# Building a graph's adjacency from one-hots on two engines instead of one

## What is computed

```python
def _genconv(x, src, dst, t, w1, b1, lg, lb, w2, b2):
    m = jax.nn.relu(x[src]) + EPS
    z = m * t
    ...
    e = jnp.exp(z - zmax[dst])
    denom = jax.ops.segment_sum(e, dst, num_segments=N)
    alpha = e / (denom[dst] + 1e-16)
    agg = jax.ops.segment_sum(alpha * m, dst, num_segments=N)
    h = agg + x
    h = jax.nn.relu(_ln(h @ w1 + b1, lg, lb))
    return h @ w2 + b2
```

## Time and profile before

| what | us |
|---|---|
| median of 3 runs (990.37 to 992.57) | 990.45 |
| the profiled execution: its own time | 991.27 |
| the profiled execution: its span | 989.4 |
| first one-hot written, from the span's start | 113.04 |
| weights of the last pair of one-hot matmuls | 201.72 |
| first aggregation of layer 0 | 211.94 |
| TensorE busy, share of the span | 92% |

### The profile page before, as it was taken

How to read it: one execution, slowest core, us unless ns; L and a number is a source line. 1 busy time by engine, 2 the same in 40 slices (tenths; PEclk the granted TensorE clock), 3 DMA queues, 4 the chain that set the end, 5 groups by cost and what they waited for, 6 DMA issues and landing times. The chain is left out here.

```text
span 989.4 us, 13105 instructions
## 1 busy us (share of the span) xinstructions
PE 912.4 (92%) x4281; PEld 666.8 (67%) x4281; DVE 707.1 (71%) x1315; ACT 445.3 (45%) x696; POOL 380.6 (38%) x326
## 2 busy tenths in 40 slices
PE   5998999979999999989999989799999999999970
PEld 3997544448887778867788777566666666666640
DVE  6856789966654676777767888588677766677765
ACT  2665000052634535435264244566565666666630
POOL 2003000016600454105531153667766666766630
PEclk9999999979999999999999999999999999999995
DMA  6433000033200222012110263599999999999868
GB/s 176 145 121 122 18 1 0 0 117 128 86 1 7 89 86 86 1 54 85 52 61 11 74 224 128 161 331 325 339 340 354 349 329 355 357 356 325 285 176 204
DMA packets 57161, 159.73 MB, mean 161 GB/s; under 512 B 13901, under 2 KB 21651, under 8 KB 48656
## 3 DMA queue, kind: packets, MB, share of 16 engines
q1 hardware_dynamic: 44725, 147.50, 43.4%
q0 software_dynamic: 12288, 11.36, 4.2%
q10 hardware_dynamic: 91, 0.13, 0.1%
HBM read 152.71 MB, written 25.58 MB: 180 GB/s over the span
## 5 line engine op out<-in xcount | busy, mean ns | idle before, releaser
L259 PE MATMUL ps<-split_operands 128*125 128x512 f32 (+5 forms) x690 | 266.2, 386 | 16.2 <-DVE split_operands L1256 5.4
L260 PE MATMUL ps<-split_operands 128*125 128x512 f32 (+5 forms) x690 | 260.4, 377 | 0.0
L261 PE MATMUL ps<-split_operands 128*125 128x512 f32 (+5 forms) x690 | 260.1, 377 | 0.0
L653 POOL DMA_INDIRECT yrow_scratch<-work,row_i x64 | 151.6, 2369 | 95.4 <-ACT work L953 92.8
L259 PEld LDWEIGHTS ps<-split_operands 128*125 128x125 f32 (+3 forms) x690 | 129.5, 188 | 45.3 <-issue 9.6
L1470 DVE TENSOR_TENSOR gate_up_lo<-expert_weights,split_operands 128x2048 fp32r<-128x2048 f32 x64 | 147.0, 2297 | 0.5 <-ACT split_operands L935 0.5
L261 PEld LDWEIGHTS ps<-split_operands 128*125 128x125 f32 (+3 forms) x690 | 129.5, 188 | 26.5
L391 POOL TENSOR_TENSOR split_operands<-work,split_operands 128x512 fp32r<-128x512 f32 x66 | 83.5, 1293 | 162.0 <-ACT split_operands L373 153.1
L260 PEld LDWEIGHTS ps<-split_operands 128*125 128x125 f32 (+3 forms) x690 | 129.6, 188 | 23.6
L935 ACT ACTIVATE split_operands<-expert_weights 128x2048 fp32r<-128x2048 f32 x64 | 121.8, 1903 | 0.0
L1963 PE MATMUL ps<-expert_weights,work 128*117 128x512 f32 x256 | 120.3, 592 | 0.5 <-issue 0.5
(11 more groups left out here) (217 smaller groups left out, 1242.5 us busy)
## 6 DMA issues: line engine op xcount, KB each, us to landing
expert_weights<-experts_in SPq DMA_DIRECT2D x64, 1024.0 KB
expert_weights<-experts_in SPq DMA_DIRECT2D x64, 512.0 KB
work<-w_in SPq DMA_DIRECT2D x12, 1024.0 KB, 5.1
yrow_scratch<-work SPq DMA_DIRECT2D x5, 1500.0 KB
split_operands<-yrow_scratch SPq DMA_DIRECT2D x4, 1120.0 KB
work<-cw_in SPq DMA_DIRECT2D x3, 1024.0 KB, 5.2
work<-rows_in SPq DMA_DIRECT2D x10, 256.0 KB, 4.6
work<-wmix_in SPq DMA_DIRECT2D x4, 512.0 KB, 5.4
```

Source lines behind the costliest of these rows:

```text
L259: pe.matmul(o, a[1], b[0], start=start, stop=False)
L260: pe.matmul(o, a[0], b[1], start=False, stop=False)
L261: return pe.matmul(o, a[0], b[0], start=False, stop=stop)
L653: pool.indirect_dma_start(yrow, bass.IndirectOffsetOnAxis(ap=row_i[:, e:e + 1], axis=0), OS[e % 4], None, bounds_check=last_row, oob_is_er ...
```

## The change

The change does five things.

1. In each group the fifth source one-hot is made by ScalarE, as Relu(1 - Abs(source - node)): an Abs of 125x626 into a new buffer `apart`, then a Relu of 125x626 into the slot. VectorE makes the other four and all five destination one-hots. TensorE waits for both engines at the fifth slot. ScalarE waits for the slot to be free before it starts Abs.
2. One pair of semaphores counts slots through all tiles; the running number of groups before a tile (`before`) is made by four more one-element steps in `tile_ranges`, and every engine loads it for tiles 1 to 4. The first group of a tile stands outside the loop, and ScalarE's copies of the tile before stand behind it.
3. The buffers `srcf`, `dstf`, `iota_h` move off EP's place; the cast that makes `iota_h` moves from the kernel's start to the other preparations of the edges.
4. The global maximum is made early. ScalarE makes the exponentials of source tiles 0 and 1 and their high parts before the adjacency; what VectorE and ScalarE have to do for these two tiles stands between the last steps of the adjacency.
5. TensorE waits for `adj_lo` only ahead of the destination tiles 2 to 4.

```diff
-        srcf, dstf = [fg(12288 + 2 * CH * i, 2 * CH, p=T) for i in range(2)]
-        iota_h = FG[0:T, 12948:12948 + 313].bitcast(F16)
+        srcf, dstf = [fg(4130 + 2 * CH * i, 2 * CH, p=T) for i in range(2)]
+        iota_h = FG[0:T, 4790:4790 + 313].bitcast(F16)
+        apart = FG[0:T, 5104:5104 + 313].bitcast(F16)
...
+        def tile_values(q, j):
+
+            groups = q.value_load(lohi_i[0:1, 1, j:j + 1], min_val=1, max_val=NG - 1)
+            before = q.value_load(lohi_i[0:1, 2, j:j + 1], min_val=0, max_val=(NT - 1) * NG) if j else 0
+            return groups, before
...
+            zmax_all(0)
             pool.wait_ge(S("first_rows_in"), 64)
...
-            adj_out(0)
-            for j in range(NT):
-                if j + 1 < NT:
-                    adj_out(j + 1)
...
+            act.wait_ge(S("zmax_neg"), 1)
+            act.wait_ge(S("attn_ps"), NT)
+            for s in range(2):
+                exponential(0, s)
+            for s in range(2):
+                exponential_hi(0, s)
...
+            def last_of_group(group, lo):
+
+                act.wait_ge(S("one_hot_free"), group * G + G)
+                act.activation(apart, iota_h, ACT.Abs, scale=-1.0, bias=srcf[:, bass.ds(lo + G - 1, 1)]).then_inc(S("apart"), 1)
+                act.wait_ge(S("apart"), group + 1)
+                act.activation(one_hot_src[:, G - 1, :], apart, ACT.Relu, scale=-1.0, bias=one_c[:]).then_inc(S("last_one_hot"), 1)
+
+            for j in range(NT):
+                groups, before = tile_values(act, j)
+                lo = act.value_load(lohi_i[0:1, 0, j:j + 1], min_val=0, max_val=CH - 1)
+                last_of_group(before, lo)
+                if j >= 1:
+                    adj_to_sb(j - 1)
+                if j >= 2:
+                    adj_to_hi(j - 2)
+                with act.Fori(1, groups + 1) as q:
+                    last_of_group(before + q, lo + q * G)
+            adj_to_sb(NT - 1)
+            adj_to_hi(NT - 2)
+            weighted_hi(0, 0)
+            adj_to_hi(NT - 1)
+            weighted_hi(0, 1)
...
             dve.wait_ge(S("iota"), 3)
-            dve.tensor_copy(iota_h, iota_i)
...
             v1(dve.tensor_copy(dstf[:, 0:CH], dsti))
+            dve.tensor_copy(iota_h, iota_i)
...
-                v1(dve.tensor_scalar(lohi[:, 1, :], lohi[:, 1, :], 1.0, None, ALU.add))
+                v1(dve.tensor_scalar(lohi[:, 1, :], lohi[:, 1, :], 1.0, None, ALU.max))
+                for j in range(1, NT):
+                    v1(dve.scalar_tensor_tensor(out=lohi[:, 2, j:j + 1], in0=lohi[:, 2, j - 1:j], scalar=1.0, in1=lohi[:, 1, j - 1:j],
+                                                op0=ALU.add, op1=ALU.add))
...
                 if t == 2:
+                    zmax_neg(0)
                     tile_ranges()
...
+            def one_hots(group, lo, near):
+
+                for i in range(G):
+                    dve.wait_ge(S("one_hot_free"), group * G + i + 1)
+                    if i < G - 1:
+                        dve.tensor_scalar(one_hot_src[:, i, :], iota_h, srcf[:, bass.ds(lo + i, 1)], None, ALU.is_equal)
+                    dve.tensor_scalar(one_hot_dst[:, i, :], near, dstf[:, bass.ds(lo + i, 1)], None,
+                                      ALU.is_equal).then_inc(S("one_hot"), 1)
...
+                one_hots(before, lo, near)
+                with dve.Fori(1, groups + 1) as q:
+                    one_hots(before + q, lo + q * G, near)
                 if j >= 2:
                     adj_low(j - 2)
+            exp_times_message(0, 0)
+            exponential_lo(0, 0)
+            exp_times_message(0, 1)
             adj_low(NT - 2)
+            weighted_lo(0, 0)
+            exponential_lo(0, 1)
             adj_low(NT - 1)
+            weighted_lo(0, 1)
...
+            def count(group):
+
+                for i in range(G):
+                    pe.wait_ge(S("one_hot"), group * G + i + 1)
+                    if i == G - 1:
+                        pe.wait_ge(S("last_one_hot"), group + 1)
...
-                last.then_inc(S(f"one_hot_free{j}"), G)
...
+                if not j:
+                    last.then_inc(S("one_hot_free"), G)
...
-            adj_transpose(NT - 1)
-
-
-            pe.wait_ge(S("adj_lo"), NT)
+
             for L in range(NL):
...
+                if not L:
+                    adj_transpose(NT - 1)
                 for s, d in [(0, 0), (0, 1), (1, 0), (1, 1), (2, 0), (2, 1), (3, 0), (4, 0), (3, 1), (4, 1)]:
...
+                else:
+                    pe.wait_ge(S("adj_lo"), NT)
```

More of the change, by code:

```diff
@@ new lines, in _ @@
+            weighted_hi(0, 0)
+            adj_to_hi(NT - 1)
+            weighted_hi(0, 1)
+            for L in range(NL):
+                if L:
+                    act.wait_ge(S("zmax_neg"), L + 1)
+                for s in range(0 if L else 2, NT + 1):
+                    if s < NT:
+                        exponential(L, s)
+                    if s >= 1 and (L or s > 2):
+                        weighted_hi(L, s - 1)
+                    if s < NT:
+                        exponential_hi(L, s)
@@ L1027, in _ @@
             dve.memset(zero_c[:], 0.0)
+            dve.memset(one_c[:], 1.0)
             dve.memset(lohi[:, 0, :], -FAR)
+            dve.memset(lohi[:, 2, :], 0.0)
             dve.memset(lohi[:, 1, :], float(CH))
@@ L1166, in _, with zmax_neg @@
             pq_low(6)
+            def zmax_neg(L):
+                dve.wait_ge(S("zmax_all"), L + 1)
+                dve.tensor_scalar(zmx[:, NT + 2:NT + 3], zmx[:, NT + 1:NT + 2], -1.0, LIFT, ALU.mult, ALU.add).then_inc(S("zmax_neg"), 1)
             def tile_ranges():
@@ L1217, in _ @@
             for j in range(NT):
                 near = iota_odd[:, j // 2, :] if j % 2 else iota_h[:, cut(T * j, T + 1)]
+                groups, before = tile_values(dve, j)
                 lo = dve.value_load(lohi_i[0:1, 0, j:j + 1], min_val=0, max_val=CH - 1)
-                steps = dve.value_load(lohi_i[0:1, 1, j:j + 1], min_val=1, max_val=NG)
-                with dve.Fori(0, steps) as q:
-                    for i in range(G):
-                        dve.wait_ge(S(f"one_hot_free{j}"), q * G + i + 1)
-                        dve.tensor_scalar(one_hot_src[:, i, :], iota_h, srcf[:, bass.ds(lo + q * G + i, 1)], None, ALU.is_equal)
-                        dve.tensor_scalar(one_hot_dst[:, i, :], near, dstf[:, bass.ds(lo + q * G + i, 1)], None,
-                                          ALU.is_equal).then_inc(S(f"one_hot{j}"), 1)
+                one_hots(before, lo, near)
@@ L1697, in adj_transpose @@
                 last.then_inc(S("adj_tr"), 1)
+            def count(group):
[3 more added lines that the diff above has]
+                        pe.wait_ge(S("last_one_hot"), group + 1)
+                    for h, s0, sn in parts:
+                        last = pe.matmul(ps[0:T, 2 * (j % 2) + h, 0:sn], one_hot_dst[:, i, 0:T], one_hot_src[:, i, cut(s0, sn)],
+                                         start=False, stop=False)
+                    last.then_inc(S("one_hot_free"), 1)
             for j in range(NT):
-                steps = pe.value_load(lohi_i[0:1, 1, j:j + 1], min_val=1, max_val=NG)
+                groups, before = tile_values(pe, j)
                 if j >= 2:
@@ L1706, in _ @@
                     last = pe.matmul(ps[0:T, 2 * (j % 2) + h, 0:sn], zero_b[:, 0:T], zero_b[:, 0:sn], start=True, stop=False)
-                last.then_inc(S(f"one_hot_free{j}"), G)
-                with pe.Fori(0, steps) as q:
-                    for i in range(G):
-                        pe.wait_ge(S(f"one_hot{j}"), q * G + i + 1)
-                        for h, s0, sn in parts:
-                            last = pe.matmul(ps[0:T, 2 * (j % 2) + h, 0:sn], one_hot_dst[:, i, 0:T], one_hot_src[:, i, cut(s0, sn)],
-                                             start=False, stop=False)
-                        last.then_inc(S(f"one_hot_free{j}"), 1)
+                if not j:
+                    last.then_inc(S("one_hot_free"), G)
+                count(before)
+                with pe.Fori(1, groups + 1) as q:
+                    count(before + q)
                 for h, s0, sn in parts:
```

84 lines of the change are left out of this document (51 added, 33 removed).

## The result

| | median, us | lowest to highest | runs |
|---|---|---|---|
| kernel before, on the chips of the comparison | 997.65 | 989.39 to 1002.85 | 20 |
| kernel after | 989.27 | 982.76 to 993.02 | 20 |
| profiled execution before | 991.27 (span 989.4, mean clock 0.978) | | |
| profiled execution after | 988.73 (span 986.9, mean clock 0.976) | | |

The account below looks back on a forecast made before the run. TensorE, busy 92%, was taken as the bound, waiting in the adjacency for VectorE's one-hots. Adjacency -3.4, way in +0.45, way out -5.65 and nothing behind sum to -8.6 us: 981.8 us from 990.45, range 974 to 991.

Parts of the forecast that it names:

- ScalarE's operation: Adjacency, fifth slot: Abs and Relu, each with a bias from memory, take 0.81 us each, say 0.80.
- The loop, 27 plain groups at 2.34: Adjacency: TensorE, Abs, Relu round the single fifth slot take 2.34 us, 0.06 more per group, 1.7 us in all.
- second rival: Adjacency: ScalarE's loop is longer through hidden register work, 0.5 us a group, kernel slower at 999 us; chance 13%.
- Boundaries: Adjacency tile boundaries: four steps of 2.78 us with ScalarE's value loads, three of 2.95 us with its copies.
- The stretch from the first one-hot (113.61) to the last pair: Whole adjacency: 85.3 us against 88.7 before, a gain of 3.4 us.
- What is gained is the boundaries, not the one-hots: Adjacency: the gain is the boundaries' 1.46 us of VectorE idling; inside the fifth-slot loop nothing is gained.
- The way in: Ahead of the adjacency: 0.9 us of added VectorE steps, 0.48 covered, so the rest is late: +0.45 us.
- The way out: Last pair to first aggregation: aggregation follows the transposes at once, 206.3 in place of 211.94: -5.65 us.
- Behind it, nothing: After the first aggregation: later weight loads, splits and GpSimd's h might lack 2.0 us of cover; nothing taken.
- The rival with the clock: Adjacency: the clock falls because TensorE waits in one 1 us piece a group, adding 8.8 us: 990.7 us; chance 5%.
- VectorE stays the bound: Adjacency: ScalarE's operations and hops stay under 1.3 us, groups take 1.98 us, -18.3 in all: 972 us; chance 6%.
- the sum -8.6 us: Whole kernel: -3.4 in the adjacency, +0.45 ahead of it, -5.65 behind it make -8.6 us.

Follow-up runs that it names:

- VectorE alone: Changed kernel, but VectorE makes all five source one-hots again, counting through all tiles and early exponentials kept: 983.1 us, ratio 0.9863.
- early Abs: Changed kernel, but ScalarE waits for the free slot between Abs and Relu, not ahead of Abs: 983.06 us, ratio 0.9849.
- second trace: The changed kernel run once more with no edit, against the kernel before: 988.72 us, ratio 0.9919.
- matmuls that keep TensorE at work: Eight unread matmuls ahead of the last transpose of the normalised input, added to the kernel before (990.91 us) and the changed kernel (983.92 us), among others.
- late exponentials: Changed kernel, but all exponentials and products of layer 0 made behind the adjacency, early maximum kept: 990.35 us, ratio 0.9916.
- counting only: Changed kernel, but VectorE makes all five one-hots and layer 0's exponentials come behind the adjacency; early maximum kept: 993.22 us, ratio 0.9952.

## Why the prediction came out as it did

- **ScalarE's operation**: 0.80 taken, 0.82 measured (means of 819 and 817 ns over 35 each). Right. The rule of the Trainium skill ("ScalarE: Activation LUTs", Rules for kernel authors) that relu and its like belong on VectorE is borne out for this placing: VectorE alone is 2.6 us quicker in the adjacency. It is not borne out for the early Abs, where ScalarE's two slow operations are hidden and the adjacency is 7.1 us shorter than VectorE's own.
- **The loop, 27 plain groups at 2.34**: mis-sized. In the first tile Abs came every 2.35 us, in the four others every 2.42 to 2.45 (20 of them). That is 1.8 us, with 0.2 more for the one step of 2.59 behind the first boundary. The added 0.07 lies between TensorE's pair and Abs. Two lines of ScalarE's timeline, of the first tile and of the last:

```profile
121.20 0.82 ACT L862 ACTIVATE work<-work 125x626 f16<-125x626 f16 x1 [0.68 <-PE ps L1799]
...
194.25 0.82 ACT L862 ACTIVATE work<-work 125x626 f16<-125x626 f16 x1 [0.76 <-PE ps L1799]
```

  The same trace shows what fills it: the register work of ScalarE's queue between the end of the wait and Abs. These are the rows of Abs's line in the queue, for a window in the first tile and for one in the last (duration min/median/max, ns):

```profile
L862 ACTq FUSED_REGOPS  x5: 53/53/70, 116.4 to 125.8; - x5
...
L862 ACTq FUSED_REGOPS  x5: 126/126/131, 189.2 to 198.9; - x5
```

  126 - 53 = 73 ns, the 0.07. In the first tile the number of groups before it is a zero that is known when the program is built; from the second on it is a register that has to be added first (`before + q`). That this addition is the 73 ns is my reading of the code; no run took it away. The prediction had such work in its second rival, as "the register work behind the wait", at a size that would make the kernel slower; it is there, at 0.07 us a group.
- **Boundaries**: 4 x 2.78 and 3 x 2.95 predicted, 4 x 2.81 and 3 x 2.82 measured. Right in the sum, within 0.3 us. The trace of the changed kernel has ScalarE's value loads: with its register work one takes 0.53 to 0.57 us (the second starts 0.56 behind the first), 1.6 for the three where 1.8 was taken. The first fifth slot's weights came after 2.16, for 2.1.
- **The stretch from the first one-hot (113.61) to the last pair**: 87.2 for a predicted 85.3, against 88.7 before. So -1.5 and not -3.4; of the 1.9 missing, 1.8 is the item above. "What is gained is the boundaries, not the one-hots" is right, and the all-VectorE kernel shows it from the other side: counting gives 4.1, and the fifth one-hot on ScalarE takes 2.6 of it back.
- **The way in**: +0.45 predicted, +0.57 measured (113.04 to 113.61). Right, as far as one execution tells: the same kernel's second trace has its first one-hot at 115.54. (The 101.64 in the working is where the weight loads of the transposes start; the line in the earlier trace rows shows their matmuls, 101.74.)
- **The way out**: -5.65 predicted, 3.81 for 10.22 measured, so -6.4. The mechanism is the predicted one. The size was off by 0.75 us. 0.5 of it is that the last transposes now ran at the full clock (0.62 us of weight loads, 1.05 before), where I had left them slow; the rest lies ahead of them (204.03 - 200.82 = 3.21 us, 3.47 before). The slow aggregation matmuls, which I had left as they were, were there.
- **Behind it, nothing**: this is the step that failed. The argument watched weights and h, and these were right: the lead of 7.3 us at 204.6 was 7.7 at 567. What was left out is TensorE's wait of 2.85 us at the router, at which in some executions the clock falls and 6.5 us are paid. The forecast compared with three times of before (990.37 to 992.57) and a trace in which the clock had held there. Most times of before taken later are at 996 to 1003, and the matmuls that keep TensorE at work bring them to 991, so the three that were known had most likely missed the fall. The changed kernel's trace met it. I can't say that the change makes the fall: it is in traces of after, of the early Abs, of the late exponentials and of counting only, not in those of before and of VectorE alone, and that before meets it too is inferred from its times, from their clocks and from what the matmuls do to them, since its one trace without the matmuls shows none. The rival with the clock looked for it inside the adjacency, with a chance of 5%, where it held through the changed kernel's pauses of 0.66 us in all its three traces. (With the late exponentials it was low there for 3.4 us.)
- **The rival "VectorE stays the bound", 972 us at 6%**, was wrong for this kernel and right for the same kernel with the slot's wait one statement further down: 1.98 us a group, 77.2 us, and 974.0 with the clock held at the router. (Its sum should read 75.4 and not 75.6, which changes nothing.) I had seen that ScalarE "waits for the slot, makes Abs" and took it as given; that Abs doesn't write the slot was in the code, and the timeline could not say it.

As a ratio the sum -8.6 us came near by luck in part: the measured medians are 8.4 apart, of which 7.0 are the change; the rest would be how often each kernel meets the fall, which was not counted. In the sum, the loop's 1.9 too much was in part made good by the 0.75 too little at the way out.

## What to carry to other kernels

When work is shared with a slower engine through a single buffer, add up the loop (reader, hop, writer, hop), and then ask which of the writer's steps touches the buffer at all: everything else belongs ahead of the wait, and here that was worth 9.7 us where the sharing itself had cost 2.6. When single times of a kernel lie in two groups, look for a wait of TensorE of a few us followed by dense work, in a trace of each group, before taking a median of three as the level; a forecast from one trace carries its clock history with it. Cheap matmuls into an unread bank during such a wait took 5 to 9 us off the medians of three versions, and 2 us off a fourth in whose trace the clock had held without them.

## What the runs showed of the hardware

- Whether the granted clock falls at one and the same wait (TensorE's, ahead of four transposes) can't be read from that wait. After 2.85 us it held in the traces of before and of VectorE alone. After 2.84 us it fell to 0.50 in both traces of after and in that of early Abs, after 2.87 in that of counting only, and after 2.37 in that of the late exponentials, each time for 10 to 17 us. In after the clock was low from the wait's end on; in its second trace TensorE had been back at work for 1.9 us when it fell. With 2.1 us of matmuls put in ahead of these transposes it held in all five traces.
- At the lower level 16 router matmuls took 3.46 us for 1.86, and 32 took 6.82 for 3.61: the cost follows the clock, though the DMA share beside them was about 1.
- ScalarE's 16-bit operation from SBUF at 626 wide, with a bias from memory, took 0.82 us, what the prediction had worked out from the 32-bit rows (0.715 + 0.09 = 0.81): 16-bit data was no quicker here. The Trainium skill ("ScalarE: Activation LUTs", What ACT_TABLE_LOAD costs) has one rate for both, and the trace agrees.
- The hop from TensorE's weights of a pair to the other engine's first instruction behind a wait against a register was 0.63 to 0.64 us to ScalarE in the first tile, close to the 0.65 to VectorE, and 0.70 to 0.71 in later tiles, where the queue's register work took 126 ns and not 53.
- A load of a value from SBUF into a register of ScalarE's queue took 0.27 to 0.29 us (the very first 0.46), and 0.53 to 0.57 with the register work behind it.
